# Neighbour sums of two graph layers by seven half-size block products instead of eight

## The reference

```python
row, col, norm = _gcn_norm(edge_index, n)      # norm = dis[row] * dis[col], with self loops
h = _gcn_layer(h, row, col, norm, W1, b1, n)   # segment_sum((h @ W)[row] * norm, col) + b
h = relu(h)
h = _gcn_layer(h, row, col, norm, W2, b2, n)
h = relu(h)
h = _gcn_layer(h, row, col, norm, W3, b3, n)
```

## Time and profile before

| | |
|---|---|
| median of the runs | 1403.46 us |
| span of the profiled execution | 1400.5 us |
| TensorE busy | 1363.9 us, 97% |
| VectorE busy | 886.7 us, 63% |
| ScalarE busy | 568.6 us, 41% |
| products, then sums of layer 0 | to 584.7 us, then to 697.3 us |
| products, then sums of layer 1 | to 740.2 us, then to 852.8 us |
| products, then sums of layer 2 | to 895.7 us, then to 1017.5 us |
| granted TensorE clock in these stages | 1.00 of full speed |

### The profile page before, as it was taken

How to read it: one execution, slowest core, us unless ns; L and a number is a source line. 1 busy time by engine, 2 the same in 40 slices (tenths; PEclk the granted TensorE clock), 3 DMA queues, 4 the chain that set the end, 5 groups by cost and what they waited for, 6 DMA issues and landing times.

```text
span 1400.5 us, 26694 instructions
## 1 busy us (share of the span) xinstructions
PE 1363.9 (97%) x11285; PEld 843.1 (60%) x11285; DVE 886.7 (63%) x1381; ACT 568.6 (41%) x980; POOL 88.0 (6%) x86
## 2 busy tenths in 40 slices
PE   9889999989998999999999999999999999999998
PEld 8779898989996655544444444454444445344443
DVE  7998998999988886567555666542354223532323
ACT  2666566656554457411142113221253224422312
POOL 3120010101002110000001000011100000000000
PEclk9999999999999999999999999999999999999999
DMA  9634344335348723000002000022210222563201
GB/s 335 227 114 148 137 138 137 126 119 177 120 146 286 238 94 108 1 31 1 0 0 61 0 0 1 1 59 77 68 40 29 73 71 78 200 212 104 91 0 60
DMA packets 71333, 136.92 MB, mean 98 GB/s; under 512 B 11908, under 2 KB 24324, under 8 KB 69798
## 3 DMA queue, kind: packets, MB, share of 16 engines
q1 hardware_dynamic: 68542, 123.98, 26.8%
q0 software_dynamic: 1280, 5.77, 1.5%
q10 hardware_dynamic: 1384, 5.38, 1.1%
HBM read 81.79 MB, written 53.32 MB: 96 GB/s over the span
## 4 chain that ended last, share of the span: by engine, by line
PE 83%; DVE 11%; ACT 2%; issue 2%; DMA 1%; POOL 0%; ACTq 0%; SPq 0%; DVEq 0%; POOLq 0%
PE banks L2305 31%; PE banks L2239 13%; PE banks L2369 12%; PE banks L1255 6%; PE banks L1655 4%; DVE x_sb L894 3%; PE banks L1192 3%; PE banks L1209 2%; PE banks L1266 2%; PE banks L1166 2%; DVE x_sb L877 1%; PE banks L2183 1%; PE banks L1625 1%; PE banks L298 1%; PE banks L1643 1%
## 5 line engine op out<-in xcount | busy, mean ns | idle before, releaser
L2305 PE MATMUL banks<-g,count 128*128 128x512 f16 x1024 | 227.6, 379 | 0.5 <-DVE tiles L2571 0.5
L2305 PE MATMUL banks<-count,g 128*128 128x512 f16 x1024 | 223.6, 379 | 0.0
L2239 PE MATMUL banks<-w_parts,h_parts 128*128 128x512 f16 x960 | 215.3, 379 | 1.7 <-DVE g L2520 1.4
L2305 PEld LDWEIGHTS banks<-count,g 128*128 128x128 f16 x1024 | 99.6, 98 | 118.0
L2305 PEld LDWEIGHTS banks<-g,count 128*128 128x128 f16 x1024 | 99.7, 98 | 113.6 <-DVE tiles L2571 1.0
L2369 PE MATMUL banks<-g,part 128*128 128x512 f16 x768 | 165.9, 379 | 0.0
L2239 PEld LDWEIGHTS banks<-w_parts,h_parts 128*128 128x128 f16 x960 | 91.2, 98 | 115.4 <-issue 11.4
L894 DVE TENSOR_TENSOR x_sb<-eb_parts,x_sb 128x4096 f16<-128x4096 f16 x64 | 146.0, 2281 | 0.0
L1255 PE MATMUL banks<-x_sb 128*128 128x128 f16 x2048 | 126.9, 221 | 11.9 <-DVE x_sb L894 11.8
L1255 PEld LDWEIGHTS banks<-x_sb 128*128 128x128 f16 x2048 | 120.9, 99 | 15.3 <-DVE x_sb L894 14.2
L2369 PEld LDWEIGHTS banks<-g,part 128*128 128x128 f16 x768 | 75.1, 98 | 90.6
(11 more groups left out here) (346 smaller groups left out, 1902.5 us busy)
## 6 DMA issues: line engine op xcount, KB each, us to landing
weight_dram<-w_new SPq DMA_DIRECT2D x60, 256.0 KB, 2.6
count<-weight_dram SPq DMA_DIRECT2D x29, 512.0 KB, 7.1
qk_dram<-stage SPq DMA_DIRECT2D x64, 128.0 KB, 2.6
tiles<-x_dram SPq DMA_DIRECT2D x32, 256.0 KB, 3.5
x_dram<-tiles SPq DMA_DIRECT2D x32, 256.0 KB, 2.8
count<-in_x SPq DMA_DIRECT2D x4, 1024.0 KB, 12.8
h<-in_x SPq DMA_DIRECT2D x16, 256.0 KB, 4.3
h_dram<-h_t SPq DMA_DIRECT2D x8, 512.0 KB, 3.3
```

Of the source, the lines that this page charges most:

```text
L2239: mm = pe.matmul(out, m.h_parts[:, slot, zh, k], m.w_parts[:, zw, k], start=n == 0 and layer != 3, stop=n == len(passes) - 1)
L2305: mm = pe.matmul(m.agg_ps[:, b], lhs, rhs, start=i == 0 and z == 0, stop=i == NT - 1 and z == 1)
```

## The change

In layers 0 and 1 the four groups of target nodes are taken in two pairs (groups 0 and 2, groups 1 and 3). With the source nodes, the features and a pair's columns each halved, the product of a pair is a 2x2 block product. It is formed by seven products of half size instead of eight: some operands are blocks, some sums or differences of blocks. A step of `paired_sums` is one such product, 8 source tiles x 2 feature blocks x 2 parts = 32 matmuls of 128x512, into two banks.

- `product_hi` in layers 0 and 1 writes the scaled result in f32 to `h_t`; `combine` (VectorE) makes S1 to S4 there; `operand_hi` (ScalarE) and `operand_lo` (VectorE) write 14 operands in two parts. `product_lo` and `add_loop` leave VectorE's order.
- One buffer `mix` of 128x4096 f16 holds the mixed counts T1 to T4 in turn, each written over the last by `mix_one` to `mix_four` when TensorE has used it (`mix_used`).
- Steps use two pairs of banks in turn. Step 1's result is copied by `keep_first` (ScalarE) into `h_t` before step 3 adds to the same banks. `join` adds a bank pair to a kept value, reading the bank in steps and writing in node order; `weigh` multiplies by `dis_row` read in steps.
- The scale is one a pair, so two a layer and not four; the last `peak_row` stands after the 5th matmul of tile 1, `peak_all` after the 9th of tile 2.
- The row sums move to ScalarE (`row_sum`), the maxima (`count_peak`) to VectorE's `products` of layer 2 (eleven, after tiles 5 to 15) and its `sums` of layer 2 (five). The identity is added on GpSimd. `edge_scale` moves from layer 2's sums to layer 3's.
- Layers 1 and 2 use five banks at the start of `products`. The loads of `b3_row` and of three raw tiles (`load_raw`) wait for the end of layer 1's sums.

The core of the diff, TensorE's list and the parts of VectorE's and ScalarE's that the prediction speaks of:

```diff
+OPERANDS = (("A11", 0), ("S3", 0), ("A11", 1), ("S3", 1), ("A12", 0), ("A22", 0), ("S2", 0), ("S1", 0), ("A12", 1), ("S2", 1), ("S4", 0),
+            ("S1", 1), ("A22", 1), ("S4", 1))
+HIGHS_AFTER = {3: OPERANDS[0:1], 6: OPERANDS[1:2], 7: OPERANDS[2:3], 10: OPERANDS[3:4], 11: OPERANDS[4:5], 12: OPERANDS[5:6],
+               13: OPERANDS[6:7], 14: OPERANDS[7:8], 15: OPERANDS[8:]}
...
+            step(1, one, "A11", lambda i: m.count[:, i, h], True)
+            if pair:
+                pe.wait_ge(s["joined"], 6 * pair)
+            step(2, other, "S2", lambda i: m.mix[:, i], True, mixed("T2", 2))
+            pe.wait_ge(s["kept"], pair + 1)
+            step(3, one, "A12", lambda i: m.count[:, HT + i, h], False)
...
+    def operand_lo(layer, name, q):
+
+        hi, lo = (parted(operand(m, name, q, z)) for z in range(2))
+        dve.wait_ge(s["high"], high_mark(layer, name, q))
+        dve.tensor_tensor(lo, by_tile(full_value(m, name, q)), hi, ALU.subtract).then_inc(s["glo"], 1)
+        dve.wait_ge(s["glo"], low_mark(layer, name, q))
...
+    def last_operands(layer):
+
+        dve.wait_ge(s["ghi"], NT * (layer + 1))
+        combine(layer, "S2", 1)
+        operand_lo(layer, "S1", 0)
+        operand_lo(layer, "A12", 1)
+        operand_lo(layer, "S2", 1)
+        combine(layer, "S4", 0)
+        combine(layer, "S1", 1)
+        operand_lo(layer, "S4", 0)
+        operand_lo(layer, "S1", 1)
+        mix_one(layer, 0, 0)
+        operand_lo(layer, "A22", 1)
+        combine(layer, "S4", 1)
+        mix_one(layer, 0, 1)
...
+    def keep_first(layer, h):
+
+        act.wait_ge(s["agg"], step_mark(layer, h, 1))
+        act.wait_ge(s["glo"], low_mark(layer, "S2", 0) if h == 0 else GLO[layer + 1])
+        act.wait_ge(s["combined"], combined_mark(layer, "S4", h))
+        act.copy(by_graph(nodes(m, h, 0)), bank_pair(m, 2 * h)).then_inc(s["kept"], 1)
...
+    def join(layer, h, step, first, place, kept):
+
+        dve.wait_ge(s["agg"], step_mark(layer, h, step))
+        dve.tensor_tensor(by_graph(place), bank_pair(m, first), by_graph(kept), ALU.add).then_inc(s["joined"], 1)
+
+    def weigh(place, c, columns=2):
+
+        return dve.tensor_tensor(by_graph(place), by_graph(place), dis_columns(m, c, columns), ALU.mult).then_inc(s["fin"], 1)
...
+            dve.wait_ge(s["joined"], 6 * number + 1)
+            join(layer, h, 4, 2 * (1 - h), nodes(m, h + 2, 2), nodes(m, h, 2))
+            mix_four(layer, h, 0)
+            dve.wait_ge(s["joined"], 6 * number + 2)
+            second_sum(layer, h, 5)
+            mix_four(layer, h, 1)
...
+                split_lo(layer + 1, 0)
+                split_lo(layer + 1, 1)
+            largest(layer, h, "C11")
+            largest(layer, h, "C22")
+            second_sum(layer, h, 6)
...
+                third_sum(layer, h, 0)
+                largest(layer, h, "C12")
+                largest(layer, h, "C21 first")
+                third_sum(layer, h, 1)
+        pair_peak(layer + 1, 1)
...
+            for u in copied_at(layer, t):
+                if layer < 2:
+                    operands(layer, u)
+                else:
+                    product_lo(layer, u)
+            if layer == 2 and 5 <= t < 5 + EARLY_PEAKS:
+                count_peak(t - 5)
```

More of the change, by code:

```diff
@@ L1538, in attention_pool @@
         pool.wait_ge(s["prob"], t + 1)
+        if t == 4:
+            nums = sorted(keep.first[n].num for n in PROJECT_SEMS.split())
+            assert nums == list(range(nums[0], nums[-1] + 1))
+            pool.sem_clear(range(nums[0], nums[-1] + 1))
         pool.tensor_tensor(keep.x[:, t, :], keep.x[:, t, :], m.bo_row[:], ALU.add).then_inc(s["plus"], 1)
@@ L1907, in layers_sp @@
             load_own(0, b)
+        if layer == 2:
+            for n in range(AHEAD):
+                load_raw(n)
         if layer == 3:
@@ L2016, in split_hi @@
         if layer in (1, 2):
[L2017 removed]
+            act.activation(out, source, ACT.Copy, scale=m.h_scale[:, layer - 1, c % 2:c % 2 + 1]).then_inc(s["hi"], 1)
         else:
@@ L2147, in layers_act @@
         products(layer)
-        sums(layer)
+        if layer < 2:
+            paired_sums(layer)
+        else:
+            sums(layer)
     products(4)
@@ new lines, in combine, with await_used @@
+    def combine(layer, name, q):
+        one, two, way = {"S1": ("A22", "S1", ALU.add), "S3": ("S3", "S1", ALU.subtract), "S2": ("A22", "S2", ALU.subtract),
+                         "S4": ("S4", "S2", ALU.subtract)}[name]
+        dve.tensor_tensor(full_value(m, name, q), full_value(m, one, q), full_value(m, two, q), way).then_inc(s["combined"], 1)
+        dve.wait_ge(s["combined"], combined_mark(layer, name, q))
+    def await_used(layer, h, step, tiles):
+        if tiles < HT:
+            dve.wait_ge(s["mix_used"], used_mark(layer, h, step, tiles // 2 - 1))
+        else:
+            dve.wait_ge(s["agg"], step_mark(layer, h, step) + (step == STEPS and h == PAIRS - 1))
@@ new lines, in weigh, with second_sum @@
+    def weigh(place, c, columns=2):
+        return dve.tensor_tensor(by_graph(place), by_graph(place), dis_columns(m, c, columns), ALU.mult).then_inc(s["fin"], 1)
+    def second_sum(layer, h, step):
+        first, joined, bank = (2, 3, 2 * h) if step == 5 else (0, 4, 2 * (1 - h))
+        place = nodes(m, h + 2, first)
+        join(layer, h, step, bank, place, place if step == 5 else nodes(m, h, 2))
+        dve.wait_ge(s["joined"], 6 * (PAIRS * layer + h) + joined)
+        weigh(place, h + 2)
@@ L2686, in late_semaphores @@
     attended = dict(zip(attention, cleared))
-    over = cleared[len(attention):] + later
+    over = cleared[len(attention):] + later + [keep.first[n] for n in PROJECT_SEMS.split()]
     table = dict(zip(layers, over))
```

472 lines of the change are left out of this document (358 added, 114 removed).

## The result

| | before | after |
|---|---|---|
| median of the runs | 1401.6 us | 1407.1 us |
| span of the profiled execution | 1400.5 us | 1405.8 us |

The median before is that of five runs: the three behind the 1403.46 us given above, and two more. The ratio is 1.0036, with a 95% interval of 1.0023 to 1.0049: slower by some 5 us, where 1397.4 us and faster was forecast. The time lies 0.6 us above the range. Rows of after are to be read against those of the front; first the busy times.

What follows compares the result with a forecast made beforehand. TensorE, busy for 97% of the span, was taken as the bound. Removed work of -31.7 us plus stalls of 25.6 made -6.1: span 1394.4, plus 3.0 from span to median, 1397.4 us, range 1390.5 to 1406.5.

Steps and rivals of the forecast that it cites:

- What is removed: Layers 0 to 2: 128 fewer matmuls (-27.6 us), fewer scale exchanges (-2.1), less bank waiting (-2.0), together -31.7 us.
- Stall 1: Sums of layers 0 and 1, first pair: TensorE waits 4.1 us for the kept copy before step 3, +8.3 us.
- Stall 2: End of layers 0 and 1: TensorE waits 2.35 us for the peak behind VectorE's last work, twice, +4.7 us.
- Stall 3: Products of layers 0 and 1, around tile 11: TensorE waits for VectorE's split, 0.8 and 1.7 us, +2.5 us.
- Stall 5: Second pairs: TensorE waits for the mixes T3, 0.33 us twice, +0.7 us.
- Stall 4: Layer 2's products: maxima between splits make a tile take VectorE 3.55 us against TensorE's 2.59, +9.4 us.
- Prices: New work on VectorE and ScalarE: combinations and low parts 1.22 us, joins 1.24, weighings 2.0, copy of first product 1.02.
- B: Rival: PSUM read in steps costs like SBUF, joins 2.0 us; +8.2 us, so 1405.5 us; chance 0.15.
- C: Rival: steps cost little for the second operand, weighings 1.24 us; -4.4 us, so 1392.9 us; chance 0.12.
- D: Rival: 1024-wide f32 work on h_gcn_t costs over 1.22 us; at 2.0 a step 23 us more, 1421; chance 0.12.
- E: Rival: the maxima don't hold up layer 2's products; -9.4 us, so 1388 us; chance 0.05.
- A: The forecast itself: span 1394.4 us, median 1397.4 us, own range 1393 to 1400.6 us; chance 0.50.

Runs made afterwards that it cites:

- three together with the other form: Changed kernel with L1736 as scalar_tensor_tensor (adds still early on GpSimd), kept copy ahead of the last high part, maxima in layer 2's sums: 1378.9 us, ratio 0.9829.

## Why the prediction was wrong

*What is removed* was right: layer 1's sums took 102.1 us for 102.2 forecast, and without any stall 98.1, which is 448 matmuls of 0.2159 (96.7) and the rest of the scale exchange.

*Stall 1*, the kept copy: 4.1 forecast, 3.80 and 3.85 measured, and ended by that copy, in front of step 3. What it cost was mis-sized: in layer 0 the matmuls behind it ran at half clock and took 9.86 us instead of 7.07, a term the sum didn't have (2.8). *Stall 2*, the peak: 2.35 forecast, 2.05 measured.

*Stall 3*, the splits of the products: 1.7 forecast in layer 1 and 0.8 in layer 0, one wait of 1.55 and one of 0.57 measured, in front of the last 26 and 24 matmuls and so two to three tiles behind the place that was named. *Stall 5*, the mixes T3: 0.33 forecast, 0.17 measured in each layer. *Stall 4*, the maxima in layer 2's products: forecast 9.4, measured one wait of 0.47 and nine of 0.75, in which a tile takes 3.51 us in place of 2.59; moving them out gave back 8.9 us of stage (54.8 to 45.9), and 10.5 where the clock stayed up behind the peak too. Each tile took VectorE 3.52 us (3.55 forecast), as two successive reductions show:

```profile
867.26 2.27 DVE L3018 TENSOR_REDUCE count_max<-count 128x1 f32<-128x2048 f16 x1
869.46 0.74 DVE L2695 SCALAR_TENSOR_TENSOR h_parts<-h_gcn_t,h_scale,h_parts 128x512 f16<-128x512 f32 x1
870.12 0.74 DVE L2765 SCALAR_TENSOR_TENSOR g<-banks,g_scale,g 128x512 f16<-128x512 f32 x1
870.78 2.27 DVE L3018 TENSOR_REDUCE count_max<-count 128x1 f32<-128x2048 f16 x1
```

The 1.2 us by which this stage was longer than forecast has the clock in it: behind the peak's wait of 2.06 us it stood at 0.71 from 853 to 858 us.

*Prices*, and with them rivals B, C and D: combinations and low parts 1.22 us, joins (PSUM in steps) 1.22, weighings (SBUF in steps) 2.02, the kept copy 1.00. All three rivals are out, and E too. The result lies on D's side, but D's mechanism (1024-wide steps above 1.44 us) had no part in it. Nor had B's: its 1405.5 is the figure nearest to the result, by luck alone, for its joins of 2.0 us were measured at 1.22. Three sums of the rivals are off: C's two terms make 3.8 us and not 4.4, A's own range, from -3 and +2.5, is 1394.4 to 1399.9, and D's 23 us at 2.0 a step are 21.8 by its own rate. None bears on the outcome.

```profile
L2778 DVE TENSOR_TENSOR h_gcn_t<-h_gcn_t 128x1024 f32<-128x1024 f32 x16 | 19.6, 1223 | 1.3 <-ACT h_gcn_t L2156 1.0
...
L2900 DVE TENSOR_TENSOR h_gcn_t<-banks,h_gcn_t 128x1024 f32<-128x1024 f32 x16 | 19.5, 1220 | 6.5 <-PE banks L2485 5.0 <-ACT h_gcn_t L2217 1.5
L2904 DVE TENSOR_TENSOR h_gcn_t<-h_gcn_t,dis_row 128x1024 f32<-128x1024 f32 x8 | 16.2, 2021 | 0.3
```

*The step that failed* is one of those costed at nothing: "The identity on GpSimd ... 16 adds of 128 end some 20 us after its start, well before tile 10". That sentence asks only when the adds are done. They were done after ten microseconds, half the time forecast, long before anyone needed them. What it didn't ask is what they do to VectorE meanwhile. This one step is 8.0 of the 11.4 us (61.3 to 53.3 in two experiments that leave all else); with it right the forecast would have been 1405.4, within 0.2% of the 1403.5 it was set against. Of the rest 2.8 are the half clock in layer 0's sums. In the median the miss is 9.7 us and not 11.4: the forecast added 3.0 us from span to median, and after the change only 1.3 lie between the two. The other moves at no cost held: ScalarE's row sums took 1.03 us each and appear as nobody's wait, and layer 2's sums and layer 3's products, which the edge exchange left and entered, take 121.2 and 50.5 us for 122.0 and 50.5 before.

The Trainium skill (SBUF — State Buffer, "Who interferes with whom") has the rule: VectorE's second pair of ports is GpSimd's too and goes to one of them as a lock, tensor_scalar is among the forms that can want it, and of two engines that want it "the other fully blocks". The runs agree for tensor_scalar: 6.16 us held, 0.17 alone, and 0.16 in a form with two tensors. The Trainium skill tells the lock as lasting one instruction. In the sixteen adds of 128x128 VectorE's tensor_scalar got no turn until the last had ended; they took 0.98 us each and started 0.59 us apart, so that by their records each began before the one ahead of it had ended. But all the traces of the kernel with seven products have a second case, in which the hold did last one instruction: GpSimd's four adds of 128x512 (851.73 to 857.10 in the changed kernel), which hardly overlap, beside two small tensor_scalars of the scale exchange.

```profile
852.95 1.71 POOL L2071 TENSOR_TENSOR tiles<-tiles,b_row 128x512 f32<-128x512 f32 x1
854.36 0.32 DVE L2639 TENSOR_SCALAR line<-line 1x2 int32<-1x2 int32 x1
854.62 1.26 POOL L2071 TENSOR_TENSOR tiles<-tiles,b_row 128x512 f32<-128x512 f32 x1
855.25 0.65 DVE L2744 TENSOR_SCALAR line<-h_line,line 1x2 f32<-1x2 f32 x1
```

They take 0.16 and 0.22 us in layer 1's exchange, with GpSimd idle. Here they end at 854.68 and 855.90, as the add beside them ends (854.66 and 855.88), while the next add goes on. Whether the overlap of the small adds is what kept VectorE out between them is not shown.

An operation with two inputs in SBUF contends with a GpSimd operation that reads SBUF by the same section of the Trainium skill. What that cost was not one thing: beside the adds of 128x128 the operations of 128x512 and 128x1024 were stretched by up to 0.38 us, and the scalar_tensor_tensor of 128x3 took its usual time; beside the adds of 128x512 a tensor_tensor of 128x16 (L2756 in the kernel of three together with the other form, at 838.82) took 1.06 us in place of 0.17, to the end of the add, and in two more traces it did the same. So another form is a cure that was measured for this one place, not a rule.

What stays open: why a gap of 3.8 us is followed by half clock at one place and not at another. 3.80 did in layer 0 and 3.85 did not in layer 1 of the changed kernel; with the adds later both did; of two waits for the peak in one trace, 2.05 us was not and 2.06 was. So a kernel with these gaps moves by 0 to 2.8 us for each from clock alone, and this is what blurs the medians of the single moves: three kernels whose layer 0 had 6.9 to 8.0 us less in its products won 3.7 to 3.9 us in the median. Where the adds, the kept copy and the maxima were mended together, 29.3 us of stage gave 28.2 us in the median. Where the rest of the single moves' gain went is shown in two profiles, by the lengths of the stages behind layer 0's products: 3.2 us with the adds later and 3.1 with the other form of L1736. The profile with half of the adds early gives nothing back; it is one of the two shortest of that kernel's ten executions (1399.0 us, mean granted clock 0.990), and the longest took 1406.5 us at 0.983. The ten of the other form go the same way, from 1399.4 us at 0.989 to 1406.0 at 0.983. Which gaps were followed by half clock in those is not on record.

## What to carry to other kernels

Work that is moved to an idle GpSimd has two prices, when it is done and what it does to VectorE beside it: look up what VectorE issues in those microseconds, and which of it is a tensor_scalar. Bound the hold by the end of the run of GpSimd's instructions: in one place here it lasted so long, in another to the end of one instruction. A held instruction of 0.17 us costs as much as what is queued behind it. And a short wait of TensorE is to be priced with half clock behind it as the other bound, since that can nearly double it.

## What was not expected of the hardware

A run of sixteen adds of 128x128 on GpSimd (0.59 us apart) held a tensor_scalar of three elements for 6.16 us, and a run of eight for 1.60, each to its end; a run of four adds of 128x512 held one of two elements for 0.65, to the end of one add, while tensor_scalars and copies of one element beside it took their usual 0.13 to 0.14; a memset of 33x64 and bn_stats beside the adds of 128x128 took their usual 0.11 and 0.69. VectorE and ScalarE read PSUM in steps of eight f32 at the price of a row (1.22 and 1.00 us for 1024), while the same steps in SBUF cost 2.02. ScalarE's sum along the row comes with an instruction of its own, 0.19 us behind each of 1.03.
